# Three unread float32 matmuls on TensorE, one ahead of the first group mean and two ahead of the first image's projections

## The reference, cut to what matters

```python
# block 1: group norm, then attention over the 1024 pixels of each image
mu  = xg.mean(axis=(2, 3, 4)); var = xg.var(axis=(2, 3, 4))      # 16 groups of 8 channels
hn  = (xg - mu) * rsqrt(var + 1e-6) * norm_w + norm_b
q, k, v = conv1x1(hn, wq, bq), conv1x1(hn, wk, bk), conv1x1(hn, wv, bv)
att = softmax(einsum("bci,bcj->bij", q, k) * c ** -0.5, axis=2)
x   = x + conv1x1(einsum("bcj,bij->bci", v, att), wp, bp)
# block 2: per image a 7 x 7 filter in the frequency domain
xf    = fftshift(fft2(x, norm="ortho"))
kern  = aniso_kernels(relu(abs(xf).mean(1)[centre 7 x 7] @ w1 + b1) @ w2 + b2)
filt  = conv(stack(xf.real, xf.imag), kern)                      # zero padded
out   = ifft2(ifftshift(mix channels of filt by wr)).real + x
```

## Time and profile before

| | us |
|---|---|
| median of 3 runs | 456.28 |
| the runs | 455.68, 456.28, 458.01 |
| the profiled execution, as timed | 458.12 |
| its span, first to last instruction | 456.3 |
| TensorE (matmul) busy | 411.3, 90% of the span |
| VectorE, ScalarE, GpSimd busy | 317.2, 253.6, 233.8 |
| mean granted TensorE clock | 0.948 of full speed |

### The profile page before, as it was taken

One profiled execution on the slowest core, in us unless ns is written; L12 is line 12 of the kernel. 1 busy time (PEld: TensorE's weight loads), 2 busy tenths in 40 slices (PEclk: granted clock), 3 DMA queues, 4 the chain that ended last, 5 costly groups with the idle time before them and its releaser, 6 DMA issues.

```text
span 456.3 us, 7030 instructions
## 1 busy us (share of the span) xinstructions
PE 411.3 (90%) x2263; PEld 344.7 (76%) x2263; DVE 317.2 (70%) x575; ACT 253.6 (56%) x450; POOL 233.8 (51%) x176
## 2 busy tenths in 40 slices
PE   2669999999999999999999999999964089999995
PEld 2447788888888888888888888888744088888884
DVE  3569698768849967894995888478343833577765
ACT  1557676656747665784664677467512312355451
POOL 0566457636816754781673476276013512467562
PEclk9999999999999999999999999999989555699999
DMA  6900100100010010010001001002150000111112
GB/s 171 385 29 2 47 1 0 47 0 0 8 38 0 0 46 0 0 46 0 0 0 46 0 0 47 1 1 68 48 134 0 0 1 1 43 49 46 76 63 92
DMA packets 6094, 17.54 MB, mean 38 GB/s; under 512 B 1632, under 2 KB 2272, under 8 KB 5856
## 3 DMA queue, kind: packets, MB, share of 16 engines
q1 hardware_dynamic: 4784, 16.70, 10.7%
q10 hardware_dynamic: 1296, 0.66, 0.5%
HBM read 13.16 MB, written 4.19 MB: 38 GB/s over the span
## 4 chain that ended last, share of the span: by engine, by line
PE 84%; DVE 8%; ACT 4%; issue 1%; DMA 1%; POOL 1%
PE PS L386 63%; PE PS L452 11%; PE PS L506 7%; PE PS L497 2%; DVE NMX L1081 1%; PE PS L528 1%; ACT E L815 1%; DMA X<-in_x 1%; DVE ETL L1096 1%; DVE K L1354 1%; DVE ML L1286 1%; DVE STAT L992 1%; ACT ETH L824 0%; ACT ETH L945 0%; POOL E L1450 0%
## 5 line engine op out<-in xcount | busy, mean ns | idle before, releaser
L1450 POOL TENSOR_TENSOR E<-E,RI 128x1024 f32<-128x1024 f32 x64 | 124.6, 1948 | 112.2 <-DVE RI L1086 112.2
L1081 DVE TENSOR_REDUCE NMX<-PS 128x1 f32<-128x1024 f32 x64 | 77.9, 1216 | 35.1 <-PE PS L386 34.5
L815 ACT ACTIVATE E<-PS,NMX 128x1024 f32<-128x1024 f32 x64 | 71.5, 1117 | 36.5 <-DVE NMX L1081 36.3
L824 ACT ACTIVATE ETH<-PS 128x512 fp32r<-128x512 f32 x128 | 69.5, 597 | 34.8 <-PE PS L452 34.4
L1096 DVE TENSOR_TENSOR ETL<-PS,ETH 128x512 fp32r<-128x512 f32 x128 | 82.0, 681 | 8.5 <-ACT ETH L824 7.7
L452 PE MATMUL PS<-MISC,E 128*128 128x128 f32 x512 | 67.2, 274 | 3.7 <-POOL E L1450 2.7
L452 PEld LDWEIGHTS PS<-MISC,E 128*128 128x128 f32 x512 | 58.7, 140 | 14.8 <-POOL E L1450 5.9
L386 PE MATMUL PS<-ETH,VH 128*128 128x512 f32 x128 | 55.1, 431 | 0.4 <-DVE ETL L1096 0.4
L386 PE MATMUL PS<-ETH,VL 128*128 128x512 f32 x128 | 50.9, 397 | 0.0
L386 PE MATMUL PS<-ETL,VH 128*128 128x512 f32 x128 | 50.5, 395 | 0.0
L386 PE MATMUL PS<-KH,QH 128*128 128x512 f32 x128 | 41.5, 406 | 2.1 <-ACT E L815 1.2
(11 more groups left out here) (188 smaller groups left out, 788.9 us busy)
## 6 DMA issues: line engine op xcount, KB each, us to landing
XTF<-in_xt SPq DMA_DIRECT2D x8, 512.0 KB, 3.3
X<-in_x SPq DMA_DIRECT2D x7, 512.0 KB, 9.3
out<-X SPq DMA_DIRECT2D x7, 512.0 KB, 2.6
E<-in_gam SPq DMA_DIRECT2D x1, 1488.4 KB, 8.9
R<-in_ana SPq DMA_DIRECT2D x1, 1320.0 KB, 5.6
E<-in_syn SPq DMA_DIRECT2D x1, 752.0 KB, 4.5
X<-in_x ACTq DMA_DIRECT2D x1, 512.0 KB, 4.6
XTF<-in_syn SPq DMA_DIRECT2D x1, 512.0 KB, 5.3
```

The lines of the kernel that those rows point to most:

```text
L815: act.activation(E[:, (t % 4) * N:(t % 4 + 1) * N], s_bank(t), ACT.Exp, bias=NMX[:, t % 2:t % 2 + 1], accum_out=RS[:, t % 4:t % 4 + 1]).th ...
L824: act.activation(et[:, h, 4 * k:4 * k + 4, i * P:(i + 1) * P], bank(ET_BANK + k).rearrange("p (j n) -> p j n", j=4), ACT.Copy).then_inc(s[ ...
L1081: dve.tensor_reduce(NMX[:, t % 2:t % 2 + 1], s_bank(t), AX.X, ALU.max, negate=True)\
L1450: TT(e, e, RI[:, t % 4:t % 4 + 1].broadcast_to([P, N]), ALU.mult)\
```

## The change

A helper `unused(n)` issues n matmuls in plain float32: the stationary matrix is `avg`, the moving one the first 512 columns of `MISC`, and the result goes to PSUM bank 5 (`ET_BANK + 1`), from which nobody reads it. No instruction on another engine changes, and no semaphore is added. Bank 5 is next written by the transposes of the first attention tile, which are on TensorE too and start afresh.

```diff
+            def unused(n):
+                for _ in range(n):
+                    mm(bank(ET_BANK + 1), avg, MISC[:, 0:HALF], True, True)
+
+            unused(1)
             group_norm_mean(0, PV_BANK)
...
             mm(bank(PV_BANK)[:, 0:P], WRAW[:, 2, :], WPT, True, True)
             mm(bank(PV_BANK)[:, P:P + 1], WPT, VEC[:, 4:5], True, True).then_inc(s["p_bvp"], 1)
+            unused(2)
```

## The result

The changed kernel has a median of 455.03 us over 20 runs (449.58 to 457.63). The kernel before, measured beside it, has 458.01 over 20 runs (455.68 to 459.49), not the 456.28 of its first three. The medians are 2.98 us apart. The ratio of the fast runs is 0.9891 (95% interval 0.9861 to 0.9921), which leaves out every run more than 1.5% above a kernel's lowest and so drops the changed kernel's ordinary runs from 456.3 up; the medians of all runs, which this text uses, give 455.03 / 458.01 = 0.9935. The forecast of 455.2 came near the measured 455.03, but on a wrong base and with too small a gain: 1.1 us were forecast.

The account below looks back on a forecast made before the run. TensorE is full from image 1 on; the change touches only the start, where 12 projection matmuls run at half speed. Base 456.28 less a gain of 1.1 (from 0.7 to 1.44) gives 455.2 us; range 453.3 to 457.0.

Parts of the forecast that it names:

- The start: Up to the first scores: hidden unread matmuls raise the clock earlier for the projections, gaining 1.16 to 1.44 us.
- upper bound: Price of an unread matmul from the weight loads of the transposes: 1.84 us each, 3.7 us for the pair.
- 0.1 to 0.3 us to spare: First unread matmul ends at 6.6 to 6.8, ahead of the product with the means at 7.06; cost 0.
- 3.3 of my sum: Pair ahead of the projections: takes 3.3 us from 10.43, over at 13.7, hidden before 14.37.
- 14.7 to 16.7: Time in us when the clock rises, at the start of the projections or inside them; chance 0.66.
- two lags: Clock rises after TensorE took up work: 5.4 to 6.3 us from 14.37, and 4.3 us from 333.56.
- The base: Median of the kernel before, 456.28 us, 1.84 below its profiled execution; gain against it 0.7 to 1.44, taken as 1.1.
- So it all moves by the same amount: Everything behind the start, full on TensorE from image 1 on, moves earlier by the start's gain.
- the rival on the half-speed stretch: From 351 to 395 us: clock rise missed in step 0's mix, made up a step later; +7.0 us, chance 0.04.
- A shift of that rise within the mix: Channel mix of step 0: the rise moves by up to 3 us of half-speed work, worth 1.5 us either way.
- No earlier rise: Rival at the start: unread matmuls do not raise the clock, or it rises at 20 as before; 456.3 us, chance 0.17.
- An earlier rise still: Rival at the start: clock rises before 9.67, gaining 0.3 more, 1.7 us in all; 454.5 us, chance 0.10.

Follow-up runs that it names:

- after_gap: Changed kernel plus 2 unread matmuls ahead of the last image's second x1 transposes: median 452.58 us, against 458.89 for the kernel before.
- after_short: Changed kernel ended behind the attention, without filters and second block: median 355.24 us.
- before_short: Kernel before ended behind the attention, without filters and second block: median 357.02 us.
- before_wait2: Kernel before plus two unread VectorE maxima (1024 and 512 columns) right ahead of step 0: median 453.62 us, against 458.89 without.
- after_late: Changed kernel plus two unread VectorE maxima (1024 and 448 columns) ahead of the first row maximum: 457.29 us, against 458.18 for the kernel before.
- only_first: Changed kernel without the pair ahead of the projections, only the first unread matmul kept: median 458.02 us, against 458.18 for the kernel before.
- only_pair: Changed kernel without the first unread matmul, only the two ahead of the projections kept: median 456.27 us, against 458.18 for the kernel before.
- before_late: Kernel before plus two unread VectorE maxima (1024 and 576 columns) ahead of the first row maximum: median 459.80 us, against 458.18 without.
- after_wait: Changed kernel plus two unread VectorE maxima (1024 and 512 columns) behind the filter parameters: 455.66 us, against 458.67 for the kernel before.
- after_chain: Changed kernel plus unread matmuls in TensorE's waits behind the attention (1, 8 and 4): median 451.31 us, against 458.89 for the kernel before.
- before_gap: Kernel before plus 2 unread matmuls ahead of the last image's second x1 transposes: median 453.30 us, against 458.25 without.
- before_wait3: Kernel before plus four unread VectorE maxima, about 3.4 us, right ahead of step 0: median 461.55 us, against 457.73 without.
- before_chain: Kernel before plus unread matmuls behind the attention (2), filter parameters (8) and filter sum (4): median 450.93 us, against 458.25 without.
- before_hot: Kernel before plus unread matmuls ahead of the second x1 transposes (2), behind attention (2), filter parameters (8) and filter sum (4): 454.88 us, against 458.25.
- after_again: Changed kernel as it is, measured once more over 12 runs: median 456.51 us, against 457.73 for the kernel before.
- after_wait2: Changed kernel plus two unread VectorE maxima (1024 and 512 columns) right ahead of step 0: 453.78 us, against 458.89 for the kernel before.

## Why the prediction was wrong

**The start: right in its mechanism.** The unread matmuls were hidden, but longer than priced. The first took 2.07 us, above the 1.65 to 1.7 that I took and above its upper bound of 1.84. Its end is put at 7.14, not at 6.6 to 6.8, so nothing was left of the 0.1 to 0.3 us to spare; still the product with the means ran at 7.00. The pair took 3.76 us against the 3.3 of my sum and the 3.7 of its upper bound, and ended at 14.23 instead of 14.1 at most; the projections still start at 14.33. `QH` begins at 16.04 behind `ANH`, `QL` at 16.85, the rise came at 16.1, inside 14.7 to 16.7. That it fell inside is in part luck: in five of the ten traces with the pair it came earlier, at 8.8 to 14.6. One of the two lags behind the range was also misread, since in the kernel before TensorE took up work at 333.56 with the clock still full, until 334.4. The early rises changed little, because `ANH` holds the first `QH`: but for after_gap, the first row maximum starts at 20.7 to 21.1 in every trace with the pair and no delay at that place. Measured gain 1.66 at the first row maximum; forecast 1.16 to 1.44. The term was undersized by 0.2, because VectorE's four operations at full supply are 0.71 apart instead of 0.75 and end at 19.67 instead of 19.89. after_short against before_short has 1.78.

**The base: mis-sized.** I took the gain down from 1.16 to 1.44 to 1.1, since the median of three runs stood 1.84 below the profiled execution. Over 20 runs the median is 458.01, and the profiled 458.12 was typical. The deduction had no ground but three runs.

**"So it all moves by the same amount": this step failed.** I let the shift pass to the end unchanged, as if nothing behind it hung on its place. But when the clock falls and rises behind 330 us is not fixed to the work: in the profiled execution 1.34 us came from a fall that did not happen and 5.1 us from an early rise, and before_wait2 shows that a shift of step 0 by 1.70 us alone can be worth 5.3 us. I had seen that such a shift can matter, but in the rival on the half-speed stretch I priced one direction only: a rise a step later, +7.0. "A shift of that rise within the mix, by up to 3 us of half-speed work, is worth up to 1.5 us either way" was the wrong bound on the other side. I had excluded a rise before the mix because in the one trace TensorE was full from 375 to 395 at half clock. The runs show that it can come in the first z of step 0. Of the 15.5 - 8.5 = 7.0 us that step 0 loses at half speed, this saved 5.1 in the profiled execution. (I also called TensorE full from 370 on; it is so from 375, and waits 0.61 us at 374.) The range ended at 453.3 for the same reason; 8 of the 20 runs lie below it, though their median does not.

**Put together:** the high groups have medians of 458.2 before (117 runs) and 456.3 after (21 of 32), 1.9 apart. Most of that is the start: over the traces without a delay at that place the first row maximum starts at 22.4 in the mean without the pair and at 21.0 with it, 1.4 apart. The rest may be the fall at 334, which is rarer with the pair (below). The low group of the changed kernel is at 449.6 to 452.3, some 6 below its high one, and holds 11 of 32 against 4 of 122 runs: (0.34 - 0.03) x 6 = 1.9 more in the mean. The expected worth of the change is thus 3.6 to 3.8 us, of which the high groups' distance is one half and the more frequent early rise the other. That the pair brings the gain at the start is shown; that the more frequent early rise comes from the shift of step 0 by 1.66 us is not, since after_late undid the shift and kept 2 low runs in 12.

**The rivals.** *No earlier rise*: excluded. *An earlier rise still*: it happened in the trace of after_short, where the clock rose at 8.8 and TensorE ran the whole pair at full clock (1.96 us for the four instructions, in place of 3.76) and the first projection at 14.01, 0.3 earlier, as priced. But the row maximum started at 20.96 all the same, because `ANH` on ScalarE holds `QH`: the 0.3 was no gain. *A step missed*: its condition came true, at a far smaller price. In 5 of the 18 traces of whole kernels (only_first, only_pair, before_late, after_wait, after_gap) the clock was not back by the end of the mix of step 0. But it came back in the first z of step 1, 17.1 to 17.9 us after z of step 0 began, and not a step later: from z of step 0 to z of step 2 it takes 405.55 - 380.39 = 25.2 us in only_first and 404.60 - 380.53 = 24.1 in before, so 1.1 us were lost and not 7.0.

**What stays open.** Why step 0 of the kernel before almost always misses the early rise and that of the changed one hits it in a third of the runs. The place of step 0 in the program does not tell: z begins at 377.5 both in after, which has the early rise, and in only_pair and after_chain, which do not. The fall and rise at about 334 to 338 are in 8 of 10 traces of kernels without the pair and in 4 of 10 with it; why is open too. So is the part of the added work in before_gap and after_gap. Another fall, at 25.2 to 29.9 us (19.7 in after_gap), is in 6 of 10 traces without the pair and in 4 of 10 with it; what it costs was not measured, except in after_gap above.

## What to carry to other kernels

Idle time of TensorE ahead of a dense stage on the critical path can be filled with unread matmuls, provided that they end before the stage's inputs arrive; here a pair of 3.8 us, in an idle place of 3.7 us, brought the first row maximum forward by 1.7 us in the profiled execution and cost nothing. Where a later stage runs at half clock with TensorE full, a change that only moves it can be worth several us, so look at the groups of the runs and not at one profile, and try a pure delay before crediting the change. And take the base from many runs: the median of three was 1.7 us off.

## What the runs showed of the hardware

- A delay of 1.7 us made a kernel 5.3 us faster (before_wait2, 453.62 against 458.89), and one of 3.4 us made it 3.8 us slower (before_wait3, 461.55 against 457.73).
- TensorE can lose the clock while it is busy: in before_chain the clock fell at 367.6, 1.3 us into 63 products of 8 and 16 columns that follow each other without a gap (behind waits of 1.36 and 0.47 us), and in before_hot at 371.2, 3.0 us into them. And in before TensorE was full from 375 to 395 at a granted clock of 0.50 without getting it back.
- The moments at which the clock changes lie differently against the work in every execution: the first rise came at 16.1 in the trace of after and at 13.4 in that of after_again, the same kernel. The early rise came 1.9, 2.1, 2.8 and 3.8 us after z of step 0 began in the traces of after_wait2, before_chain, before_wait2 and after.
- A VectorE operation on 49x16 elements took 2.59 us beside a GpSimd operation of 3.48 us, and 0.88 when it began 1.9 us later beside the same one; in both it ended with the GpSimd operation, 0.03 us behind it. Two VectorE maxima over 1024 and 512 columns ran beside that operation in 1.22 and 0.68 us.
